# Attention and channel mix in one kernel: v products for two groups at a time, four probability buffers, one VectorE reduction per score chunk

## Chip, core and metric

The kernel runs on one core of one Trainium2 chip. The metric is the device time of one execution in microseconds, the median of several. A core has TensorE (PE, with weight loads shown apart as PEld), VectorE (DVE), ScalarE (ACT), GpSimd (POOL) and SyncE (SP, which issues every transfer here). Each engine takes its instructions in the order in which they were written and waits at semaphores.

## What is computed

Sixteen sequences of 512 tokens with 128 channels go through causal attention with 16 heads of 8 channels, a layer norm, a channel mix of the RWKV kind and a second layer norm:

```python
h = x @ W1 + b1                                   # q, k, v of 16 heads, d = 8
w = einsum('bhqd,bhkd->bhqk', q, k) / sqrt(8)
w = softmax(w * tril - (1 - tril) * 1e6)          # S = 512
x = layernorm(x + einsum('bhqk,bhkd->bhqd', w, v) @ Wp + bp)
xk = mu_k * x + (1 - mu_k) * x_prev               # xr likewise, with mu_r
out = sigmoid(xr @ W_r.T) * (relu(xk @ W_k.T) ** 2 @ W_v.T)
x = layernorm(x + out)
```

## The kernel before

**Stages and steps.** The work on one sequence passes six stages, and a step of the program works on several sequences at once, each in another stage: X (transpose x), A (q and k), S (scores with queries on the partitions, to find each row's maximum), T (the scores again with keys on the partitions, exponential, product with v), D (sums, projection, first layer norm), E (channel mix, second norm). `run_steps` runs 21 steps. A step is divided into ten groups g = 0 to 9 (two halves of five, `c` = g mod 5) and a group into four chunks i = 0 to 3. The text writes "g4" for group 4.

**A chunk.** `scores(b, par, g, i)` writes one PSUM bank of S scores (`sps`, L493, at most 512 columns in one or two matmuls, then two small mask matmuls L505 and L507) and one bank of T scores (`tps`, L473). S and T have three banks each (`BANKS = 3`). DVE reduces a bank of S to row maxima (`reduce_chunk`: L687 for chunks of one or two parts, L691 for the last group of a half). ACT turns a bank of T into probabilities (`exp_chunk_of`, L616). PE may write chunk n only once chunk n - 3 has been read. `max_unit` says which blocks an S chunk holds: a chunk with u even is one block row of 512 columns; one with u odd ("short") holds block row 2 (384 columns) and block row 0 (128 columns), which DVE reduces in two instructions.

**Masks and v.** POOL zeroes the diagonal blocks of a group's probabilities (`mask_group(b, g)`, L777, one instruction in an even c and two in the others) after the fourth exponential of the group. PE then multiplies by v (`pv(b, ..., g)`, L537, four or eight matmuls in float32, four of them side by side on strips of 32 columns), accumulating a half's five groups in the bank `ops`. `probs` has two buffers, by g mod 2. The call is at the end of each group: `pv` of group g - 1 after the chunks of group g, and `pv` of group 9 in g0 of the next step.

**The rest of the work** shares one PSUM bank, `spare`. The table `SPARE_USES[(g, place)]` sets when each use comes on PE: place 0 after chunks 0 and 1, place 1 after chunks 2 and 3. Each use waits until the one before it was read. Those that matter here:

- (0, 1) q and (1, 1) k: PE writes `spare` (L399), ACT makes the high part (L595), DVE reads `spare` once more for the rest (`qk_rest`, L715);
- (2, 0) key (L399 with `mixed`), read by ACT; (2, 1) sums1 (L440), normalised by DVE into `attn` (a reciprocal and four L725);
- (3, 0) gate (L413), read by ACT (L607); (3, 1) attnT (L443); (4, 1) value (L407); (5, 0) project; (5, 1) v;
- (6, 0) max0, (6, 1) xT, (8, 0) hT (L450), (8, 1) sums0.

**GpSimd's own order** in a step ends with: masks of g6 (L777), split of the maxima, h normalised in g7 (L804), masks of g7, the second norm's deviation, half of the result, masks of g8, the other half, `step_d` (`mix_step`, L811), masks of g9. ACT scales `step_d` twice (`scale_steps`, L633) at the end of g9, ahead of the exponentials of the next g0. In g3 POOL adds the bias to a reloaded x (`xbias`, L835), which waits for the transfer of `xres`, and stands ahead of the masks of g3.

Of the kernel before, what the change touches and what calls it, by code (L numbers as in the profile page):

```python
# [11 lines left out]
P = 128  # L12
# [10 lines left out]
QUARTET = 4  # L23
TERMS = 6 * DH
# [36 lines left out]
def bank_free(n):  # L61

    return n + 1 - BANKS

# [61 lines left out]
def diagonals(ap, u):  # L126


    if u < 2 * QUARTET:
        return ap[:, (2 if u % 2 else 3) * BLK:].rearrange("p (j w) -> p j w", w=BLK)  # L130
    return ap.rearrange("p (j w) -> p j w", w=2 * BLK)[:, :, BLK:]


def block_program(nc, x, W1, b1, Wp, bp, Wr, Wk, Wv, mu_r, mu_k, consts, half_rows, out):
    with ExitStack() as ctx:
# [96 lines left out]
        s_reduced = sem("s_reduced")  # L232
        max_high = sem("max_high")
# [139 lines left out]
        def _(pe):  # L373
# [19 lines left out]
            def rowmax_transpose(par, half):  # L393
                src = rowmax[:, par, QUARTET * half:QUARTET * half + QUARTET].rearrange("p t h a -> p (t h a)")
                return nc.tensor.transpose(spare[0:MAXIMA, 0:P], src, ident)
# [21 lines left out]
            def spare_use(b, par, g, place):  # L417
# [12 lines left out]
                elif use == "max0":  # L430
                    wait(pe, s_reduced, 4 * GROUPS * before("S", b) + 2 * GROUPS)
                    last = rowmax_transpose(1 - par, 0)
                elif use == "max1":
                    wait(pe, s_reduced, 4 * GROUPS * (before("T", b) + 1))
                    last = rowmax_transpose(par, 1)
# [85 lines left out]
            def pv(b, entries, par, g):  # L521
# [11 lines left out]
                for k in range(per_pair):  # L533
                    for t in range(QUARTET):
# [4 lines left out]
                                                probs[:, g % 2, i, off:off + w],  # L539
# [3 lines left out]
            def step(b, par):  # L543
                for g in range(GROUPS):
# [13 lines left out]
        def _(act):  # L558
# [51 lines left out]
            def exp_chunk_of(b, g, i):  # L610
                n = before("T", b)
                half, c = divmod(g, CHUNKS)
                if i == 0:
                    wait(act, pv_done, GROUPS * n + g - 1)
                wait(act, t_done, 4 * GROUPS * n + 4 * g + i + 1)
                nc.scalar.activation(probs[:, g % 2, i, :], tps[:, bank(4 * GROUPS * n + 4 * g + i), :], ACT.Exp, scale=SCALE)\  # L616
# [42 lines left out]
        def _(dve):  # L659
# [19 lines left out]
            def reduce_chunk(b, par, g, i):  # L679
# [5 lines left out]
                if u < 2 * QUARTET:  # L685
                    for t, a, off, w in max_unit(u):
                        last = nc.vector.reduce_max(rowmax[:, par, QUARTET * half + t, hh, a:a + 1],  # L687
                                                    sps[:, bank(n), off:off + w], axis=AX_X)
                else:
                    pair = QUARTET * half + max_unit(u)[0][0]  # L690
                    last = nc.vector.reduce_max(rowmax[:, par, pair:pair + 2, hh, 1],  # L691
                                                sps[:, bank(n), :].rearrange("p (j w) -> p j w", j=2), axis=AX_X)
                last.then_inc(s_reduced, 1)

# [10 lines left out]
            def spare_use(b, par, g, place):  # L705
# [11 lines left out]
                elif use in ("sums0", "sums1"):  # L717
# [43 lines left out]
        def _(pool):  # L761
# [9 lines left out]
            def mask_group(b, g):  # L771
# [3 lines left out]
                for _, _, _, off, _ in exp_chunk(g % CHUNKS, 0):  # L775
                    v = probs[:, g % 2, :, off:off + BLK]
# [128 lines left out]
```

## Time and profile before

| | |
|---|---|
| time, median of 3 | 714.41 us (711.55 to 716.44) |
| the profiled execution | 715.99 us, its span 714.3 us |
| busy in the span | PE 84%, DVE 74%, ACT 65%, POOL 61% |
| mean granted TensorE clock | 0.944 of full speed |
| 80 to 120 us and the steady steps | granted clock 1.00 |
| a steady step | 37.5 us, some of them 38 to 39 us |

The page of the profile gives sums over the whole span; the core fills up to about 120 us, has steps of equal length until about 640 us, and drains. A step is therefore read from the timeline of each engine in one stretch (394.0 to 431.5 us is used below), in which each row is one or more instructions of one kind: start, length from the first start to the last end, engine, line, what is written and read, count, and in brackets how long the engine had been idle and for whom. Records of matmuls overlap, so a PE that waits only a little shows no bracket: what tells is the distance from one row's start to the next row's.

### The profile page before, as it was taken

The page shows a single profiled execution, that of the slowest core. Times are in us where ns is not written, and L with a number is a line of the kernel's source. Part 1 is how long each engine was busy: PE and PEld are TensorE (multiplying, and loading weights), DVE is VectorE, ACT ScalarE, POOL GpSimd, SP SyncE. Part 2 cuts the span into 40 slices and gives each one's busy share as a digit, 9 for nine tenths or more (in the row PEclk, how much of TensorE's full clock was granted, in tenths as well). Part 3 has the DMA queues.
Part 4 walks back from the last instruction along what each step waited for, and adds up shares of the span by engine and source line. Part 5 has one row for each costly group of instructions (what it writes and reads, how often), then busy time and mean ns, then how long its engine had stood idle before and what let it go on. Part 6 is the DMA issues. An engine that isn't in the chain of part 4 may idle for free.

```text
span 714.3 us, 19231 instructions
## 1 busy us (share of the span) xinstructions
PE 599.9 (84%) x7405; PEld 321.4 (45%) x7405; DVE 530.4 (74%) x1388; ACT 464.6 (65%) x918; POOL 439.0 (61%) x680
## 2 busy tenths in 40 slices
PE   2359997999999999998989999899999998988623
PEld 1025453545454545454545454454545454533311
DVE  3058887889898888888898989797988888832121
ACT  1210776686878787778687777778687767676410
POOL 6110434467677676868676858576767767667653
PEclk9995899999999999999999999999999999989655
DMA  1332323132322323232323232415142332000100
GB/s 56 86 94 89 106 65 108 44 120 49 97 86 66 118 62 122 62 121 62 121 55 121 52 112 62 109 46 135 48 104 79 66 102 64 18 17 17 31 15 15
DMA packets 63615, 53.63 MB, mean 75 GB/s; under 512 B 8730, under 2 KB 59292, under 8 KB 63524
## 3 DMA queue, kind: packets, MB, share of 16 engines
q1 hardware_dynamic: 63524, 52.41, 26.2%
q8 instruction: 58, 0.95, 0.6%
q14 instruction: 33, 0.27, 0.1%
HBM read 34.82 MB, written 17.30 MB: 73 GB/s over the span
## 4 chain that ended last, share of the span: by engine, by line
PE 35%; POOL 25%; DVE 13%; ACT 11%; issue 10%; DMA 3%; SPq 2%; POOLq 0%; DVEq 0%; ACTq 0%
PE ops L537 9%; PE sps L493 7%; POOL probs L777 6%; PE spare L399 6%; ACT probs L616 5%; DVE rowmax L687 5%; POOL rstd L799 4%; POOL h L804 4%; POOL result L804 4%; PE spare L413 3%; PE spare L407 3%; PE tps L473 2%; POOL step_d L811 2%; DVE qk_rest L715 2%; DVE stats L698 2%
## 5 line engine op out<-in xcount | busy, mean ns | idle before, releaser
L616 ACT ACTIVATE probs<-tps 128x512 f32<-128x512 f32 x640 | 341.7, 598 | 125.6 <-PE tps L473 125.4
L687 DVE TENSOR_REDUCE rowmax<-sps 128x1 f32<-128x512 f32 (+2 forms) x768 | 337.7, 503 | 53.8 <-PE sps L507 52.0
L777 POOL TENSOR_SCALAR_AFFINE_SELECT probs<-probs 128x512 f32<-128x512 f32 x256 | 157.7, 633 | 157.5 <-ACT probs L616 157.0
L493 PE MATMUL sps<-kop,qop 52*128 52x384 bf16 (+3 forms) x1024 | 220.2, 310 | 34.3 <-DMA kop<-d_parts 13.8
L473 PE MATMUL tps<-qop,kop 54*128 54x128 bf16 (+3 forms) x1024 | 219.5, 304 | 12.6 <-ACT probs L616 12.6
L537 PE MATMUL ops<-probs,vop 128*32 128x384 f32 (+3 forms) x2048 | 172.7, 444 | 8.7 <-POOL probs L777 6.3
L493 PEld LDWEIGHTS sps<-kop,qop 52*128 52x128 bf16 x1024 | 71.3, 95 | 158.3 <-DVE rowmax L687 86.5
L505 PE MATMUL sps<-qmask,rows_of 64*128 64x128 bf16 (+1 forms) x640 | 134.3, 212 | 0.0
L507 PE MATMUL sps<-qmask,rows_of 64*128 64x128 bf16 (+1 forms) x640 | 131.8, 208 | 0.0
L691 DVE TENSOR_REDUCE rowmax<-sps 128x2 f32<-128x512 f32 x128 | 79.5, 684 | 13.7 <-PE sps L507 12.7
L537 PEld LDWEIGHTS ops<-probs,vop 128*32 128x32 f32 x2048 | 55.3, 110 | 73.1 <-issue 46.0
L473 PEld LDWEIGHTS tps<-qop,kop 54*128 54x128 bf16 x1024 | 69.2, 94 | 26.3 <-ACT probs L616 24.7
L507 PEld LDWEIGHTS sps<-qmask,rows_of 64*128 64x128 bf16 x640 | 62.5, 99 | 21.5 <-issue 3.4
L505 PEld LDWEIGHTS sps<-qmask,rows_of 64*128 64x128 bf16 x640 | 61.5, 97 | 16.1 <-issue 2.4
L784 POOL TENSOR_TENSOR qk_parts<-qk_rest,qk_parts 128x512 bf16<-128x512 f32 x32 | 36.8, 1152 | 35.3 <-ACT qk_parts L627 35.3
L715 DVE SCALAR_TENSOR_TENSOR qk_rest<-spare,bias,qk_parts 128x512 f32<-128x512 f32 x32 | 24.0, 751 | 29.4 <-ACT qk_parts L595 29.4
L835 POOL TENSOR_TENSOR xbias<-xres,bias 128x512 f32<-128x512 f32 x16 | 20.3, 1267 | 34.0 <-DMA xres<-L_attn_x 34.0
L817 POOL TENSOR_TENSOR mixed<-scaled,hT 128x512 f32<-128x512 f32 x32 | 40.0, 1268 | 0.8 <-ACT scaled L633 0.8
L595 ACT ACTIVATE qk_parts<-spare,bias 128x512 bf16<-128x512 f32 x32 | 21.8, 680 | 28.1 <-PE spare L399 27.5
L399 PE MATMUL spare<-xT,w1p 128*32 128x512 f32 x256 | 37.6, 662 | 2.3 <-DVE qk_rest L715 1.6
L799 POOL TENSOR_TENSOR rstd<-vareps,half_power 128x4 f32<-128x4 f32 x32 | 33.4, 1043 | 2.7
L738 DVE SCALAR_TENSOR_TENSOR gated<-gate,spare 128x512 f32<-128x512 f32 x16 | 11.0, 687 | 30.8 <-PE spare L407 30.8
(75 smaller groups left out, 650.0 us busy)
## 6 DMA issues: line engine op xcount, KB each, us to landing
d_parts<-qk_parts SPq DMA_DIRECT2D x16, 768.0 KB, 3.9
qop<-d_parts SPq DMA_DIRECT2D x192, 32.0 KB
qop<-d_parts SPq DMA_DIRECT2D x64, 96.0 KB
kop<-d_parts SPq DMA_DIRECT2D x192, 32.0 KB
kop<-d_parts SPq DMA_DIRECT2D x64, 96.0 KB
xa<-L_attn_x SPq DMA_DIRECT2D x16, 256.0 KB, 3.0
xres<-L_attn_x SPq DMA_DIRECT2D x16, 256.0 KB, 3.4
out<-result SPq DMA_DIRECT2D x16, 256.0 KB, 2.5
```

Source lines behind the costliest of these rows:

```text
L399: last = nc.tensor.matmul(spare[32 * m:32 * m + 32, :], weights[:, 32 * m:32 * m + 32], tokensT, start=True, stop=True, skip_group_check=True)
L473: last = nc.tensor.matmul(tps[:, bank(n), off:off + w], kop[r, par, pair, BLK * a:BLK * a + BLK], qop[r, par, pair, BLK * a:SEQ], start=Tr ...
L493: nc.tensor.matmul(sps[:, bank(n), off:off + w], qop[r, par, pair, BLK * a:BLK * a + BLK], kop[r, par, pair, 0:w], start=j == 0, stop=Fals ...
L505: nc.tensor.matmul(out[:, :, 0:HROWS], rows_of[r, 0, :], rhs, start=False, stop=False, skip_group_check=True)
L507: nc.tensor.matmul(out[:, :, HROWS:], rows_of[r, 1, :], rhs, start=False, stop=True, skip_group_check=True).then_inc(s_done, 1)
L537: last = nc.tensor.matmul(ops[32 * t:32 * t + 32, BLK * a:SEQ], vop[:, par, a, QUARTET * half + t, hh, :], probs[:, g % 2, i, off:off + w] ...
L616: nc.scalar.activation(probs[:, g % 2, i, :], tps[:, bank(4 * GROUPS * n + 4 * g + i), :], ACT.Exp, scale=SCALE)\
L687: last = nc.vector.reduce_max(rowmax[:, par, QUARTET * half + t, hh, a:a + 1], sps[:, bank(n), off:off + w], axis=AX_X)
L691: last = nc.vector.reduce_max(rowmax[:, par, pair:pair + 2, hh, 1], sps[:, bank(n), :].rearrange("p (j w) -> p j w", j=2), axis=AX_X)
L777: last = nc.gpsimd.affine_select(out=v, in_=v, compare_op=ALU.is_ge, fill=0.0, base=0, pattern=[[0, QUARTET], [1, BLK]], channel_multiplie ...
L799: nc.gpsimd.tensor_tensor(rstd[:, i, :], vareps[:, i, :], half_power[:], ALU.pow).then_inc(done_rstd, 1)
L804: last = nc.gpsimd.tensor_scalar(dst[:, t, :], src[:, t, :], negmean[:, i, t:t + 1], rstd[:, i, t:t + 1], ALU.add, ALU.mult)
```

## The change

1. **Product with v in pairs.** A table sets after which group which products are done: `PV_AFTER = {2: (0, 1), 4: (2, 3), 5: (4,), 7: (5, 6), 9: (7, 8)}`; that of group 9 stays in g0 of the next step. `probs` has four buffers in place of two, and the exponentials of a group wait for the product four groups back.
2. **Short S chunks** are laid out as block row 0 first, then block row 2 (384 columns), and one DVE instruction reduces the bank as four blocks of 128 columns, so that `rowmax` gets a new axis of four: blocks of a short chunk are a row's own maximum (block row 0) and three partial ones (block row 2). Once in each half, after the second chunk of its last group, a small DVE reduction over the three partial maxima of eight head rows completes them (`block2_done`), and the transposes of the maxima wait for it.
3. **attn** is made by one DVE instruction of 128x256 in place of four of 128x64.

```diff
+PBUFS = 4
+PV_AFTER = {2: (0, 1), 4: (2, 3), 5: (4,), 7: (5, 6), 9: (7, 8)}
...
-            return [(t, 2, 0, 3 * BLK), (t, 0, 3 * BLK, BLK)]
+            return [(t, 0, 0, BLK), (t, 2, BLK, 3 * BLK)]
...
-        rowmax = sb("rowmax", [P, 2, PAIRS, 2, NQBLK])
+        rowmax = sb("rowmax", [P, 2, NQBLK, PAIRS, 2, NQBLK])
...
-        probs = sb("probs", [P, 2, QUARTET, SEQ])
+        probs = sb("probs", [P, PBUFS, QUARTET, SEQ])
...
                     if g == 0 and active("D", b):
                         pv(b, before("D", b), 1 - par, GROUPS - 1)
-                    elif g > 0 and active("T", b):
-                        pv(b, before("T", b), par, g - 1)
+                    for done in PV_AFTER.get(g, ()):
+                        if active("T", b):
+                            pv(b, before("T", b), par, done)
...
                 if i == 0:
-                    wait(act, pv_done, GROUPS * n + g - 1)
+                    wait(act, pv_done, GROUPS * n + g + 1 - PBUFS)
...
-                if u < 2 * QUARTET:
-                    for t, a, off, w in max_unit(u):
-                        last = nc.vector.reduce_max(rowmax[:, par, QUARTET * half + t, hh, a:a + 1],
-                                                    sps[:, bank(n), off:off + w], axis=AX_X)
...
+                elif u % 2 == 0:
+                    last = nc.vector.reduce_max(rowmax[:, par, 0, pair, hh, 3:], sps[:, bank(n), :], axis=AX_X)
                 else:
...
+                    last = nc.vector.reduce_max(rowmax[:, par, :, pair, hh, 0],
+                                                sps[:, bank(n), :].rearrange("p (j w) -> p j w", w=BLK), axis=AX_X)
                 last.then_inc(s_reduced, 1)
+                if c == CHUNKS - 1 and i == 1:
+
+                    wait(dve, s_reduced, n - 1)
+                    of = rowmax[:, par, :, QUARTET * half:QUARTET * half + QUARTET].rearrange("p j t h a -> p a (t h) j")
+                    nc.vector.reduce_max(of[:, 2, :, 0], of[:, 0, :, 1:], axis=AX_X).then_inc(block2_done, 1)
...
-                    for t in range(TT):
-                        last = nc.vector.tensor_tensor(
-                            attn[:, t, DH * half:DH * half + DH].rearrange("q (r h) d -> q r h d", h=2),
-                            tiles[:, 0, t], inv[:, half, t].unsqueeze(3).to_broadcast([P, QUARTET, 2, DH]), ALU.mult)
-                    last.then_inc(spare_read, 1)
+                    nc.vector.tensor_tensor(
+                        attn[:, :, DH * half:DH * half + DH].rearrange("q t (r h) d -> q t r h d", h=2), tiles[:, 0],
+                        inv[:, half].unsqueeze(4).to_broadcast([P, TT, QUARTET, 2, DH]), ALU.mult).then_inc(spare_read, 1)
```

How the program reads on the engines. First TensorE, from k (`spare<-xT,w1p`, end of g1) to key (`spare<-mixed,wffT`, middle of g2), before:

```order
L399 MATMUL spare<-xT,w1p 32x512 x4
L537 MATMUL ops<-probs,vop 32x512 x4
L493 MATMUL sps<-kop,qop 128x512
L473 MATMUL tps<-qop,kop 128x512
L505 MATMUL sps<-qmask,rows_of 128x64
L507 MATMUL sps<-qmask,rows_of 128x64
L493 MATMUL sps<-kop,qop 128x512
L473 MATMUL tps<-qop,kop 128x512
L505 MATMUL sps<-qmask,rows_of 128x64
L507 MATMUL sps<-qmask,rows_of 128x64
L399 MATMUL spare<-mixed,wffT 32x512 x4
```

and now, on the same engine at the same place (line numbers are those of the changed kernel):

```order
L405 MATMUL spare<-xT,w1p 32x512 x4
L501 MATMUL sps<-kop,qop 128x512
L481 MATMUL tps<-qop,kop 128x512
L513 MATMUL sps<-qmask,rows_of 128x64
L515 MATMUL sps<-qmask,rows_of 128x64
L501 MATMUL sps<-kop,qop 128x512
L481 MATMUL tps<-qop,kop 128x512
L513 MATMUL sps<-qmask,rows_of 128x64
L515 MATMUL sps<-qmask,rows_of 128x64
L405 MATMUL spare<-mixed,wffT 32x512 x4
```

The product with v of group 0 (four matmuls) has gone from between k and key. TensorE at the end of g2, from the last short chunk to the first chunk of g3, before:

```order
L493 MATMUL sps<-kop,qop 128x384
L473 MATMUL tps<-qop,kop 128x512
L493 MATMUL sps<-kop,qop 128x128
L505 MATMUL sps<-qmask,rows_of 128x2x64
L507 MATMUL sps<-qmask,rows_of 128x2x64
L440 MATMUL spare<-cst,osum 128x128 x4
L537 MATMUL ops<-probs,vop 32x384 x4
L537 MATMUL ops<-probs,vop 32x128 x4
L493 MATMUL sps<-kop,qop 128x512
```

and now:

```order
L501 MATMUL sps<-kop,qop 128x128
L481 MATMUL tps<-qop,kop 128x512
L501 MATMUL sps<-kop,qop 128x384
L513 MATMUL sps<-qmask,rows_of 128x2x64
L515 MATMUL sps<-qmask,rows_of 128x2x64
L448 MATMUL spare<-cst,osum 128x128 x4
L545 MATMUL ops<-probs,vop 32x512 x4
L545 MATMUL ops<-probs,vop 32x384 x4
L545 MATMUL ops<-probs,vop 32x128 x4
L501 MATMUL sps<-kop,qop 128x512
```

The product of group 0 now stands here, ahead of that of group 1, and the small part of the short chunk is written first. VectorE from g6 to the end of g9 and into g0, before:

```order
L687 TENSOR_REDUCE rowmax<-sps 128x1 x16
L722 RECIPROCAL inv<-spare 128x32
L725 TENSOR_TENSOR attn<-spare,inv 128x64 x4
L691 TENSOR_REDUCE rowmax<-sps 128x2 x4
L687 TENSOR_REDUCE rowmax<-sps 128x1 x6
```

and now:

```order
L702 TENSOR_REDUCE rowmax<-sps 128x4 x2
L738 RECIPROCAL inv<-spare 128x32
L740 TENSOR_TENSOR attn<-spare,inv 128x4x64
L696 TENSOR_REDUCE rowmax<-sps 128x2 x2
L709 TENSOR_REDUCE rowmax<-rowmax 128x8
L696 TENSOR_REDUCE rowmax<-sps 128x2 x2
L699 TENSOR_REDUCE rowmax<-sps 128x1 x2
L702 TENSOR_REDUCE rowmax<-sps 128x4 x2
```

A short chunk is one reduction of 128x4 where it was two of 128x1, `attn` is one instruction, and the small reduction stands in the middle of the last group of the half.

## Rows read from the trace of the kernel before

**Rows 1.** Stretches: us, busy of PE, PEld, DVE, ACT, POOL; clock, DMA

```profile
394.01:431.48 37.47, 34.89 (x468) 19.16 (x463) 32.78 (x87) 28.78 (x58) 26.67 (x43) 1.00 0.29 85
431.48:470.28 38.80, 35.08 (x467) 19.10 (x463) 32.77 (x87) 28.78 (x58) 26.64 (x42) 1.00 0.32 88
281.17:545.42 264.25, 244.75 (x3239) 133.85 (x3235) 229.42 (x603) 201.45 (x400) 186.49 (x294) 1.00 0.32 87
```

**Rows 2.** Timeline of TensorE from k to key: start, length, what

```profile
412.12 1.06 PE L399 MATMUL spare<-xT,w1p 128*32 128x512 f32 x8
413.00 1.04 PE L537 MATMUL ops<-probs,vop 128*32 128x512 f32 x8
413.97 0.39 PE L493 MATMUL sps<-kop,qop 52*128 52x512 bf16 x1
...
414.85 1.07 PE L399 MATMUL spare<-mixed,wffT 128*32 128x512 f32 x8 [0.21 <-DVE qk_rest L715]
```

**Rows 3.** Timeline of ACT and DVE in the same stretch

```profile
413.34 0.67 ACT L595 ACTIVATE qk_parts<-spare,bias 128x512 bf16<-128x512 f32 x1
414.05 0.75 DVE L715 SCALAR_TENSOR_TENSOR qk_rest<-spare,bias,qk_parts 128x512 f32<-128x512 f32 x1 [0.50 <-ACT qk_parts L595]
```

**Rows 4.** Timeline of TensorE from attnT to the product of group 3

```profile
420.67 0.66 PE L443 MATMUL spare<-cst,attn 128*128 128x128 f32 x4
421.26 1.07 PE L537 MATMUL ops<-probs,vop 128*32 128x512 f32 x8
422.26 0.28 PE L493 MATMUL sps<-kop,qop 52*128 52x256 bf16 x1
...
424.88 1.05 PE L537 MATMUL ops<-probs,vop 128*32 128x384 f32 x16
```

**Rows 5.** Timeline of POOL, ACT and PE from g6 to the next g0

```profile
396.15 1.23 POOL L777 TENSOR_SCALAR_AFFINE_SELECT probs<-probs 128x512 f32<-128x512 f32 x2 [2.13 <-ACT probs L616]
405.17 1.03 POOL L811 TENSOR_TENSOR step_d<-hT 128x512 f32<-128x512 f32 x1
406.24 1.33 ACT L633 ACTIVATE scaled<-step_d,mus 128x512 f32<-128x512 f32 x2 [0.60 <-POOL step_d L811]
408.11 0.39 PE L473 MATMUL tps<-qop,kop 54*128 54x512 bf16 x1 [0.73 <-ACT probs L616]
```

**Rows 6.** Timeline of DVE in g6 to g8, and of PE in g9

```profile
395.91 6.74 DVE L687 TENSOR_REDUCE rowmax<-sps 128x1 f32<-128x384 f32 x16
...
404.37 0.28 PE L493 MATMUL sps<-kop,qop 52*128 52x256 bf16 x1 [0.23 <-DVE rowmax L691]
404.81 1.07 PE L537 MATMUL ops<-probs,vop 128*32 128x384 f32 x16
```

**Rows 7.** DVE's groups by shape, 281.17 to 545.42 us: busy, mean ns

```profile
L687 DVE TENSOR_REDUCE rowmax<-sps 128x1 f32<-128x512 f32 x113 | 72.5, 683 | 6.9 <-PE sps L507 6.5
L687 DVE TENSOR_REDUCE rowmax<-sps 128x1 f32<-128x384 f32 x112 | 61.2, 546 | 8.9 <-PE sps L507 8.4
L687 DVE TENSOR_REDUCE rowmax<-sps 128x1 f32<-128x128 f32 x112 | 31.3, 279 | 0.0
L725 DVE TENSOR_TENSOR attn<-spare,inv 128x64 f32<-128x64 f32 x56 | 8.6, 216 | 0.5
```

**Rows 8.** Timeline of DVE: attn, two short chunks, g4

```profile
418.11 0.61 DVE L725 TENSOR_TENSOR attn<-spare,inv 128x64 f32<-128x64 f32 x4
420.46 1.42 DVE L687 TENSOR_REDUCE rowmax<-sps 128x1 f32<-128x384 f32 x4 [0.46 <-PE sps L507]
422.80 2.48 DVE L691 TENSOR_REDUCE rowmax<-sps 128x2 f32<-128x512 f32 x4 [0.92 <-PE sps L507]
```

**Rows 9.** Waits over the span, and the timeline of one late transfer

```profile
PE ops L537 <- POOL probs L777: 6.3, 4, 3.5
...
461.14 1.29 POOL L835 TENSOR_TENSOR xbias<-xres,bias 128x512 f32<-128x512 f32 x1 [3.29 <-DMA xres<-L_attn_x]
463.65 1.07 PE L537 MATMUL ops<-probs,vop 128*32 128x384 f32 x16 [1.13 <-POOL probs L777]
```

More of the change, by code:

```diff
@@ L129, in diagonals @@
     if u < 2 * QUARTET:
-        return ap[:, (2 if u % 2 else 3) * BLK:].rearrange("p (j w) -> p j w", w=BLK)
+        blocks = ap.rearrange("p (j w) -> p j w", w=BLK)
+        return blocks[:, 0:NQBLK:3] if u % 2 else blocks[:, 3:]
     return ap.rearrange("p (j w) -> p j w", w=2 * BLK)[:, :, BLK:]
@@ L393, in rowmax_transpose @@
             def rowmax_transpose(par, half):
-                src = rowmax[:, par, QUARTET * half:QUARTET * half + QUARTET].rearrange("p t h a -> p (t h a)")
+                src = rowmax[:, par, 0, QUARTET * half:QUARTET * half + QUARTET].rearrange("p t h a -> p (t h a)")
                 return nc.tensor.transpose(spare[0:MAXIMA, 0:P], src, ident)
@@ L431, in spare_use @@
                     wait(pe, s_reduced, 4 * GROUPS * before("S", b) + 2 * GROUPS)
+                    wait(pe, block2_done, 2 * before("S", b) + 1)
                     last = rowmax_transpose(1 - par, 0)
@@ L434, in spare_use @@
                     wait(pe, s_reduced, 4 * GROUPS * (before("T", b) + 1))
+                    wait(pe, block2_done, 2 * (before("T", b) + 1))
                     last = rowmax_transpose(par, 1)
@@ L613, in exp_chunk_of @@
                 if i == 0:
-                    wait(act, pv_done, GROUPS * n + g - 1)
+                    wait(act, pv_done, GROUPS * n + g + 1 - PBUFS)
                 wait(act, t_done, 4 * GROUPS * n + 4 * g + i + 1)
-                nc.scalar.activation(probs[:, g % 2, i, :], tps[:, bank(4 * GROUPS * n + 4 * g + i), :], ACT.Exp, scale=SCALE)\
+                nc.scalar.activation(probs[:, (GROUPS * n + g) % PBUFS, i, :], tps[:, bank(4 * GROUPS * n + 4 * g + i), :], ACT.Exp, scale=SCALE)\
                     .then_inc(exp_done, 1)
@@ L684, in reduce_chunk @@
                 wait(dve, s_done, n + 1)
-                if u < 2 * QUARTET:
-                    for t, a, off, w in max_unit(u):
-                        last = nc.vector.reduce_max(rowmax[:, par, QUARTET * half + t, hh, a:a + 1],
-                                                    sps[:, bank(n), off:off + w], axis=AX_X)
-                else:
-                    pair = QUARTET * half + max_unit(u)[0][0]
-                    last = nc.vector.reduce_max(rowmax[:, par, pair:pair + 2, hh, 1],
-                                                sps[:, bank(n), :].rearrange("p (j w) -> p j w", j=2), axis=AX_X)
+                pair = QUARTET * half + max_unit(u)[0][0]
+                if u >= 2 * QUARTET:
+                    last = nc.vector.reduce_max(rowmax[:, par, 0, pair:pair + 2, hh, 1],
+                                                sps[:, bank(n), :].rearrange("p (j w) -> p j w", j=2), axis=AX_X)
+                elif u % 2 == 0:
+                    last = nc.vector.reduce_max(rowmax[:, par, 0, pair, hh, 3:], sps[:, bank(n), :], axis=AX_X)
+                else:
+                    last = nc.vector.reduce_max(rowmax[:, par, :, pair, hh, 0],
+                                                sps[:, bank(n), :].rearrange("p (j w) -> p j w", w=BLK), axis=AX_X)
                 last.then_inc(s_reduced, 1)
+                if c == CHUNKS - 1 and i == 1:
+                    wait(dve, s_reduced, n - 1)
+                    of = rowmax[:, par, :, QUARTET * half:QUARTET * half + QUARTET].rearrange("p j t h a -> p a (t h) j")
+                    nc.vector.reduce_max(of[:, 2, :, 0], of[:, 0, :, 1:], axis=AX_X).then_inc(block2_done, 1)
             def layer_norm_moments(src, i, n, ready, value, done_stats, done_moments):
```

5 lines of the change are left out of this document (3 added, 2 removed).

## Prediction

> **What bounds the kernel now.** I read the stretches first. In a steady step of 37.47 us TensorE has 34.89 us of records, VectorE 32.78, ScalarE 28.78, GpSimd 26.67, at a granted clock of 1.00, which is 2.4 GHz [rows 1]. No engine is full: VectorE has 37.47 - 32.78 = 4.7 us of idle time per step, and TensorE's figure flatters it, since its records overlap. So a sum per engine does not answer the question, and I followed one step in the timelines, asking at each place what released the instruction that everything after it stands behind. Three kinds of stretch came out.
>
> First, the chain of `spare` from k to key. PE writes k from 412.12 and is free for the next work at 413.00 [rows 2]. ACT reads it at 413.34, DVE at 414.05, done at 414.80 [rows 3]; key starts at 414.85 [rows 2]. In between PE does the product of group 0 (413.00 to 413.97) and two chunks of g2, and then still waits 0.21 us. This product lies wholly in the shadow of the chain k, ACT, DVE, key.
>
> Second, from key to the end of g5, PE's own order: sums1, the product of group 1, gate, attnT, the product of group 2 (421.26 to 422.26), g4, value, the product of group 3 at 424.88 [rows 4], project, v, the product of group 4. Here a microsecond of PE is a microsecond of the step.
>
> Third, from g6 to the next g0, GpSimd: the masks of g6 start when the exponentials of g6 are there (396.15, after 2.13 us of idleness) and GpSimd then has no gap until `step_d` ends at 405.17 + 1.03 = 406.20; ACT scales from 406.24, and only then come the exponentials of g0, so that the T matmul of its fourth chunk starts at 408.11 after 0.73 us of waiting [rows 5]. The distance 396.15 to 408.11, 11.96 us, is one chain. VectorE is nearly as tight there: 16 reductions without a gap from 395.91 for 6.74 us, and in g9 PE waits for it (404.37) before it comes to the product of group 7 [rows 6].
>
> **The change, part by part.**
>
> *Product of group 0, moved from g1 to g2.* At its old place it cost nothing. Without it PE does the two chunks of g2 about a microsecond earlier and then waits for the same `qk_rest`: key still starts at 414.85. At its new place, behind sums1, it stands in the second kind of stretch. Its price: float32 work followed by float32 work takes 412.12 to 413.00 = 0.88 us for the same number of columns, and followed by scores 413.00 to 413.97 = 0.97 or 421.26 to 422.26 = 1.00 [rows 2, 4]. In a pair the first product is of the former kind, 0.88. So **+0.88 us** per step. ACT and DVE have no work of the old shadow that could use the time: both stand in the chain.
>
> *Product of group 2, moved from g3 to g4.* g4 starts its 1.00 us earlier, value and the product of group 2 follow, and that of group 3 after 0.88 us: 0.88 - 1.00 = **-0.12 us**. Both places lie in the second stretch.
>
> *Products 5 and 7, moved from g6 to g7 and g8 to g9.* Here the third stretch decides, and PE has room: what counts is whether it comes late for GpSimd's chain. After the last chunk of a group DVE holds three banks, 3 x 0.60 = 1.8 us of work: four reductions take 2.48 us with the last one's 0.68, so they lie 0.60 apart [rows 7, 8]. A pair of products takes 0.88 + 1.00 = 1.88 us, and a chunk reaches DVE about 0.5 us after PE begins it (422.26 to 422.80 is 0.54 [rows 4, 8]). DVE idles about 0.8 us behind each pair, where a single product left it none. Walking g7 to g0 by these distances: g7 begins 1.0 us earlier and g8 0.8 us later than now, the third and fourth exponentials of g8 end about 0.1 us later, as does what GpSimd has behind the masks of g8; g9's fourth chunk starts 0.2 us later (404.6 in place of 404.37), the pair begins at 405.0 and ends at 406.9, its scores reach ACT at 407.4, and ACT is busy with `scaled` until 407.5 anyway [rows 5, 6]. The pair's second microsecond in g9 is hidden by the 0.73 us for which PE waited at 408.11 [rows 5] and by what ACT still had to do. I take **+0.1 us**; the bounds are 0 (GpSimd's chain hides all) and +1.0 (the pairs' idle times on DVE add up there, 2 x 0.8 less what DVE saves).
>
> *The short chunk's order.* Small part first puts the 384 columns behind the T matmul. Where T waits (408.11), the S part after it is 384 instead of 128 columns long: 256 columns at 2.4 GHz, **+0.1 us**. Elsewhere both row halves carry the same 512 columns.
>
> *One reduction per short chunk.* Two short chunks take 1.42 us, 0.71 with the tail; the four instructions' last is 0.28 long, so a chunk is 0.66 apart against 0.60 for one 512-column reduction [rows 7, 8]. A four-block reduction is not in the trace; the nearest is L691's two blocks, 0.60 apart like one block, and I take 0.60 (bounds 0.60 and 0.66). Sixteen short chunks a step: -0.96 us of DVE work.
>
> A page speaks against this size. The Trainium skill, "VectorE: DVE Perf Modes", section "The TRN2 errata", gives an instruction that reads PSUM a fixed 120 cycles at 0.96 GHz; by it an instruction less would be 0.125 us, the sixteen 2.0 us. The trace has 0.06 each, since an instruction starts before the one ahead has ended, and the trace decides.
>
> *attn.* Four take 0.61 us. One of 256 elements: 216 ns + 192 x (683 - 279) / 384 ns = 0.42 us [rows 7, 8]; twice, -0.38 us. *Small reduction:* 24 elements, below 0.28 us (128 elements), I take 0.17, twice, +0.34 us; its data are done two chunks earlier, so its wait costs nothing. DVE in all: -0.96 - 0.38 + 0.34 = -1.0 us of 32.8. **On the path: 0.** In the first and second stretch DVE has idle time (0.46 and 0.92 us ahead of the rows at 420.46 and 422.80 [rows 8]), in the third GpSimd's chain is as long and gets nothing. The cover is thin there, so the bound is -1.0.
>
> *Four buffers.* The exponentials' wait for the product two groups back shows nowhere; what ended ACT's idle time was T scores or, at one place, `step_d`. Worth 0. They are what lets the pairs be.
>
> *Late transfers.* The product of group 3 needs the masks of g3, which stand behind `xbias` and so behind the transfer of `xres`. Where that is late (461.14), PE waits, and the step is 38.80 us instead of 37.47; over the run 6.3 us in four places, the longest 3.5 [rows 1, 9]. SP issues the transfer at the same time as before, while PE comes to the product of group 3 later by 0.88 (product 0) and 0.88 (product 2 ahead of it), 1.76 us. That recovers 6.3 less about 1.7 of the longest, 4.6; I take **-4 us** for the run.
>
> *Sum.* +0.88 - 0.12 + 0.1 + 0.1 = 0.96 us per step in which q and k are made beside T and the channel mix's neighbours are there, 13 steps: +12.5 us. With -4 it is +8.5. The profiled execution took 715.99 us, so 724.5; it lay 1.6 us above the median of the three, so **723 us**, 1.2% slower.
>
> **The rivals.**
>
> *Faster: DVE is what paces the kernel after all.* For it: 32.78 of 37.47 us busy, no gap in g6 to g8, PE waiting for it in g9 [rows 1, 6]. Then a step loses 1.0 us of DVE work and the microsecond of product 0 lies beside it, and four pairs save 4 x 0.12 us of switching: -1.5 x 15 steps = -22, 692 us; if only the third stretch goes by DVE, half of its saving counts, about -0.5 x 14 - 4 against nothing added, 704. Against it: 4.7 us of DVE idle time per step and a GpSimd chain of 11.96 us that no part of the change shortens [rows 1, 5]. It decides if `step_d` ends with POOL having had gaps. Chance 0.20. By the page's 0.125 us per instruction the same rival would give 2.0 - 0.96 = 1.0 us more a step.
>
> *No difference: only the late transfers and a part of the microsecond.* The shadow moves: g2's chunks come earlier and the second stretch has places where PE waits a little, so that product 0 costs 0.4 rather than 0.88. (0.4 - 0.12 + 0.1) x 13 - 4 = +1, 715 us; this region, 711 to 719, gets 0.22.
>
> *Much slower: the pairs starve DVE and ACT.* If behind the pairs of g7 and g9 the idle times are not hidden (bound +1.0 above instead of +0.1): (0.96 + 0.9) x 13 - 4 = +20, 735 us. It decides if DVE's idle time behind the pair of g7 pushes sums0 later by more than GpSimd's order does. For it: the slack in my walk is only about 0.2 us. Chance 0.16.
>
> **How the numbers follow.** My forecast has 0.42, with its own range of 718 to 728. A measurement of this kernel tells about 1% from no change (the three runs span 0.7%). Over 1% faster is below 707.3: the faster rival but its edge, 0.18. Over 1% slower is above 721.6: the much slower rival and 0.32 of the forecast's 0.42, 0.48. Between: 0.34. The range for 8 in 10 leaves out the full DVE gain and the far end of starving: 704 to 733.
>
> **What the profile after would show.** Key starts as long after k as before (2.73 us), with PE idle for about a microsecond ahead of it and no product between. From key to the first chunk of g6 the step is 0.8 us longer. GpSimd still runs without a gap from the masks of g6 to `step_d`, and 12.0 to 12.2 us lie between those masks and the T matmul of g0's fourth chunk. Short chunks are reduced in 0.68 us, 0.60 apart, DVE busy near 31.8 us per step with more idle time, and PE waits for POOL ahead of a product hardly ever. A steady step is 38.4 us. I am wrong if a steady step is below 37.5 us: then a place that I took for GpSimd's or PE's was DVE's; or above 39, then the pairs starve what follows them.

## The result: 731.8 us, 2.7% slower

The changed kernel takes 731.82 us (median of four, 729.49 to 733.61), against 715.04 us for the kernel before on the same chip. The ratio is 1.0267, with a 95% interval of 1.0237 to 1.0297. The direction and the cost of moving product 0 were forecast; falls of TensorE's clock were not: +8.6 us were predicted and +16.8 came. The profiled execution took 730.78 us, its span is 728.5 us.

From the page of the changed kernel, its sums over the span:

```profile
span 728.5 us, 18909 instructions
PE 599.4 (82%) x7405; PEld 327.8 (45%) x7405; DVE 508.6 (70%) x1068; ACT 463.3 (64%) x918; POOL 439.4 (60%) x680
```

DVE has 320 instructions and 22 us of work less than before, PE the same work, and the kernel is slower. The stretches of the changed kernel from one `step_d` to the next, and a part of the second (columns as in [rows 1]):

```profile
371.71:409.97 38.26, 34.36 (x466) 19.42 (x462) 31.39 (x67) 28.71 (x58) 26.68 (x43) 1.00 0.32 85
409.97:449.87 39.90, 36.00 (x466) 19.73 (x462) 31.38 (x67) 28.71 (x58) 26.71 (x44) 0.96 0.27 83
441.20:444.70 3.50, 3.50 (x28) 1.02 (x28) 1.28 (x3) 0.57 (x1) 3.35 (x9) 0.53 0.05 9
```

There are two kinds of step. The common one takes 38.26 us; before it was 37.46 (the stretch of 37.47 in [rows 1]). The other kind takes 39.7 to 39.9 us, with the same instructions on every engine, DVE and ACT as busy as in the first kind, but the granted clock at 0.96, and at 0.53 between 441.2 and 444.7. TensorE ran there at 1.2 GHz instead of 2.4. In the kernel before, the granted clock is 1.00 from 130 to 632 us; its first fall after that (0.50 from 634 to 640 us) comes where the core already drains.

TensorE's timeline in the changed kernel, from k to the pair of g2, then the pair of g7 in either kind of step:

```profile
378.71 1.06 PE L405 MATMUL spare<-xT,w1p 128*32 128x512 f32 x8
379.71 0.39 PE L501 MATMUL sps<-kop,qop 52*128 52x512 bf16 x1
...
381.45 1.06 PE L405 MATMUL spare<-mixed,wffT 128*32 128x512 f32 x8 [1.07 <-DVE qk_rest L731]
...
383.82 1.93 PE L545 MATMUL ops<-probs,vop 128*32 128x512 f32 x24
...
397.69 0.39 PE L501 MATMUL sps<-kop,qop 52*128 52x512 bf16 x1
...
401.29 0.39 PE L501 MATMUL sps<-kop,qop 52*128 52x512 bf16 x1 [0.79 <-DVE rowmax L702]
...
402.92 1.93 PE L545 MATMUL ops<-probs,vop 128*32 128x512 f32 x24
...
441.24 3.50 PE L545 MATMUL ops<-probs,vop 128*32 128x512 f32 x24
```

Key still starts 2.74 us after k (381.45 - 378.71; 2.73 in [rows 2]), now with 1.07 us of waiting ahead of it. From key to the first chunk of g6 it is 397.69 - 381.45 = 16.24 us, against 430.37 - 414.85 = 15.52 before: +0.72. The same pair of products takes 1.93 us at 402.92 and 3.50 us at 441.24. In the profiled execution this happened five times up to 640 us, at 171.98, 441.24, 557.91, 597.43 and 635.84 us, always at the pair of g7. A sixth fall, at 654.56 us, is in the drain, at the pair of g2; every kernel here, the one before too, has falls after 626 us.

GpSimd in the changed kernel, masks of g6 and `step_d`, and DVE's two waits in that stretch:

```profile
400.93 1.23 POOL L791 TENSOR_SCALAR_AFFINE_SELECT probs<-probs 128x512 f32<-128x512 f32 x2 [2.13 <-ACT probs L625]
...
409.97 1.03 POOL L825 TENSOR_TENSOR step_d<-hT 128x512 f32<-128x512 f32 x1
```

```profile
405.26 1.29 DVE L699 TENSOR_REDUCE rowmax<-sps 128x1 f32<-128x512 f32 x2 [1.04 <-PE sps L515]
...
411.95 1.29 DVE L699 TENSOR_REDUCE rowmax<-sps 128x1 f32<-128x512 f32 x2 [0.94 <-PE sps L515]
```

GpSimd's chain is 9.04 us from masks to `step_d`, as before (9.02, [rows 5]). DVE idles a microsecond behind each of the two pairs, and these two microseconds cost nothing in this kernel. The T matmul of g0's fourth chunk starts at 412.90, 11.97 us after the masks of g6; before it was 11.96.

DVE's groups by shape in the changed kernel, 284 to 560 us:

```profile
L702 DVE TENSOR_REDUCE rowmax<-sps 128x4 f32<-128x512 f32 x116 | 74.1, 681 | 6.0 <-PE sps L515 6.0
...
L740 DVE TENSOR_TENSOR attn<-spare,inv 128x256 f32<-128x256 f32 x14 | 5.9, 425 | 0.5
...
L709 DVE TENSOR_REDUCE rowmax<-rowmax 128x8 f32<-128x24 f32 x14 | 2.7, 190 | 0.0
```

### The profile page after: what moved, and what is told of

It is laid out like the page before. It is cut to its first block, busy times and chain, and to the rows that moved or that the text cites. A ratio compares the mean times of both kernels' runs of the same rounds, so it can differ in the third digit from the quotient of the medians.

```text
span 728.5 us, 18909 instructions
## 1 busy us (share of the span) xinstructions
PE 599.4 (82%) x7405; PEld 327.8 (45%) x7405; DVE 508.6 (70%) x1068; ACT 463.3 (64%) x918; POOL 439.4 (60%) x680
## 4 chain that ended last, share of the span: by engine, by line
PE 44%; DVE 29%; ACT 9%; POOL 8%; issue 5%; DMA 3%; SPq 2%; DVEq 0%; POOLq 0%; ACTq 0%
PE ops L545 17%; DVE rowmax L699 10%; PE sps L501 8%; DVE rowmax L702 7%; PE spare L405 5%; ACT probs L625 4%; DVE stats L714 3%; PE spare L419 3%; PE spare L413 3%; PE tps L481 3%; POOL probs L791 2%; DVE rowmax L696 2%; DVE qk_rest L731 2%; ACT qk_parts L604 2%; DVE moments L718 1%
## 5 line engine op out<-in xcount | busy, mean ns | idle before, releaser
L501 PE MATMUL sps<-kop,qop 52*128 52x128 bf16 (+3 forms) x1024 | 222.2, 311 | 50.0 <-DVE rowmax L702 12.7
L699 DVE TENSOR_REDUCE rowmax<-sps 128x1 f32<-128x512 f32 x256 | 164.5, 684 | 91.7 <-PE sps L515 91.7
L702 DVE TENSOR_REDUCE rowmax<-sps 128x4 f32<-128x512 f32 x256 | 163.7, 682 | 11.7 <-PE sps L515 11.6
L545 PE MATMUL ops<-probs,vop 128*32 128x384 f32 (+3 forms) x2048 | 165.0, 452 | 3.7 <-POOL probs L791 3.7
L501 PEld LDWEIGHTS sps<-kop,qop 52*128 52x128 bf16 x1024 | 71.5, 95 | 144.0 <-DVE rowmax L702 43.5
L545 PEld LDWEIGHTS ops<-probs,vop 128*32 128x32 f32 x2048 | 61.7, 113 | 94.4 <-issue 76.0
L696 DVE TENSOR_REDUCE rowmax<-sps 128x2 f32<-128x512 f32 x128 | 82.1, 684 | 0.7
L515 PEld LDWEIGHTS sps<-qmask,rows_of 64*128 64x128 bf16 x640 | 62.8, 99 | 37.7 <-issue 6.1
L405 PE MATMUL spare<-xT,w1p 128*32 128x512 f32 x256 | 38.4, 676 | 2.4 <-DVE qk_rest L731 1.6
L405 PE MATMUL spare<-mixed,wffT 128*32 128x512 f32 x128 | 18.8, 661 | 21.1 <-DVE qk_rest L731 12.8
```

Source lines behind the costliest of these rows:

```text
L405: last = nc.tensor.matmul(spare[32 * m:32 * m + 32, :], weights[:, 32 * m:32 * m + 32], tokensT, start=True, stop=True, skip_group_check=True)
L501: nc.tensor.matmul(sps[:, bank(n), off:off + w], qop[r, par, pair, BLK * a:BLK * a + BLK], kop[r, par, pair, 0:w], start=j == 0, stop=Fals ...
L515: nc.tensor.matmul(out[:, :, HROWS:], rows_of[r, 1, :], rhs, start=False, stop=True, skip_group_check=True).then_inc(s_done, 1)
L545: last = nc.tensor.matmul(ops[32 * t:32 * t + 32, BLK * a:SEQ], vop[:, par, a, QUARTET * half + t, hh, :], probs[:, (GROUPS * entries + g) ...
L696: last = nc.vector.reduce_max(rowmax[:, par, 0, pair:pair + 2, hh, 1], sps[:, bank(n), :].rearrange("p (j w) -> p j w", j=2), axis=AX_X)
L699: last = nc.vector.reduce_max(rowmax[:, par, 0, pair, hh, 3:], sps[:, bank(n), :], axis=AX_X)
```

## The experiments

Every kernel ran beside the kernel before. The length of a step is the distance between two starts of `step_d` in a profiled execution. Beside the changed kernel the kernel before took 715.04 us, beside experiments 1 to 4 712.23, beside 5 to 8 713.95, beside 9 and 10 713.24; so across these groups the ratios compare better than the times.

**1. Products alone again, all else kept.**

```diff
-PV_AFTER = {2: (0, 1), 4: (2, 3), 5: (4,), 7: (5, 6), 9: (7, 8)}
+PV_AFTER = {1: (0,), 2: (1,), 3: (2,), 4: (3,), 5: (4,), 6: (5,), 7: (6,), 8: (7,), 9: (8,)}
```

> The changed kernel with its table set back to one product per group, at the ends of g1 to g9 as before; the DVE changes, the short chunks' order and the four buffers stay. My theory (product 0 out of the shadow of k and key, plus TensorE's clock at 1.2 GHz in five places at the paired products of g7; DVE's saving hidden): a steady step of 37.5 us, no fall of the clock in the steady steps, 714 us (712 to 717). Rival, DVE paces the kernel: 1.0 us less a step, 700 us. Rival, the new order of the short chunk or the small reduction costs: over 720 us.

Measured: 718.58 us, ratio to before 1.0086 (1.0044 to 1.0127). The step is 37.52 us:

```profile
370.00 1.03 POOL L825 TENSOR_TENSOR step_d<-hT 128x512 f32<-128x512 f32 x1
407.53 1.03 POOL L825 TENSOR_TENSOR step_d<-hT 128x512 f32<-128x512 f32 x1
```

Without the pairs 1.8 of the 2.7% are gone (13 us of 17 by the medians), and in the steady steps the clock does not fall. DVE's microsecond per step is worth nothing at this placement: 37.52 is no less than 37.46. The time is 4.6 us above what I expected. The kernel is still 0.9% (6 us) slower than the one before, although the steps account for 0.06 us each; experiments 7 and 10 come back to it.

**2. Pairs alone, on the kernel before.** `PV_AFTER` and the four buffers put into the kernel before; DVE as before.

```diff
-probs = sb("probs", [P, 2, QUARTET, SEQ])
+probs = sb("probs", [P, PBUFS, QUARTET, SEQ])
...
-                    elif g > 0 and active("T", b):
-                        pv(b, before("T", b), par, g - 1)
+                    for done in PV_AFTER.get(g, ()):
+                        if active("T", b):
+                            pv(b, before("T", b), par, done)
```

> The kernel before with nothing but the pairs and the four probability buffers. My theory: all of the loss comes with the pairs, so a steady step of 38.2 us, falls of the clock at the pair of g7, and 731 us (727 to 735) or a few us more, since DVE is 1.0 us slower per step. Rival, the loss is the DVE part's: 715 us. Rival, DVE's saving is worth something once PE feeds it in bursts: 740 us or more.

Measured: 744.56 us, ratio 1.0465 (1.0406 to 1.0525), the third reading. A step without a fall of the clock is 38.7 us against 38.26 with the new DVE part, and there were seven falls between 200 and 640 us instead of four. DVE's timeline in this kernel, its waits behind the pair of g4 and behind the pair of g7 in a step with a fall:

```profile
403.95 1.29 DVE L692 TENSOR_REDUCE rowmax<-sps 128x1 f32<-128x512 f32 x2 [1.30 <-PE sps L511]
...
417.48 2.66 DVE L692 TENSOR_REDUCE rowmax<-sps 128x1 f32<-128x512 f32 x6 [2.59 <-PE sps L511]
```

DVE idles 1.30 us behind the pair of g4 (1.21 in the changed kernel, at 393.66), and 2.59 us behind that of g7, since the pair itself runs at half the clock. The value of DVE's saving depends on where TensorE's bursts are: nothing with single products, 0.44 us per step and three falls of the clock with pairs. My expectation (731, or a few more) missed this.

**3. Product 0 back between k and key, pairs at g4, g7, g9.**

```diff
-PV_AFTER = {2: (0, 1), 4: (2, 3), 5: (4,), 7: (5, 6), 9: (7, 8)}
+PV_AFTER = {1: (0,), 2: (1,), 4: (2, 3), 5: (4,), 7: (5, 6), 9: (7, 8)}
```

> The changed kernel with product 0 alone put back to the end of g1, where it stands between k and key; pairs at g4, g7, g9 stay. My theory: 0.7 us per step come back, the step is 37.5 us, the clock still falls at g7 in some steps at 1.6 us each: 719 us (715 to 723). Rival, pairs as such starve DVE and ACT: the step stays at 38.0 or more, 726 us or more.

Measured: 719.18 us, ratio 1.0101 (1.0049 to 1.0153); steps of 37.40 to 37.6 us, and two falls of the clock before 640 us, both after 580 us. The pairs of g4, g7 and g9 do not lengthen a step. The expectation held, 719 us and 37.5 us a step.

**4. The pair of g7 apart.** Product 5 at the end of g6, product 6 at g7; product 0 stays moved.

```diff
-PV_AFTER = {2: (0, 1), 4: (2, 3), 5: (4,), 7: (5, 6), 9: (7, 8)}
+PV_AFTER = {2: (0, 1), 4: (2, 3), 5: (4,), 6: (5,), 7: (6,), 9: (7, 8)}
```

> The changed kernel with the pair of g7 taken apart alone: product 5 back at the end of g6, product 6 at the end of g7. My theory: the step stays 38.2 us, since product 0 is still out of the shadow, but TensorE works through g6 and g7 as before and its clock stays at 2.4 GHz in the steady steps: 723 us (720 to 726), five falls at 1.6 us gained. Rival, the falls come from the kernel's slower pace as a whole: they stay, 731 us.

Measured: 722.52 us, ratio 1.0157 (1.0112 to 1.0202). The steps are 38.24 us, all of them, and the clock is whole from 120 to 640 us:

```profile
120.00:640.00 520.00, 465.29 (x6258) 260.26 (x6258) 426.97 (x896) 387.04 (x770) 357.74 (x567) 1.00 0.31 82
```

That is 9.3 us less than the changed kernel by the medians, and 1.1% (7.9 us) by the ratios, with the same regular step; five falls at 39.90 - 38.26 = 1.64 us would be 8.2.

**5. Only product 0 moved.**

```diff
-PV_AFTER = {1: (0,), 2: (1,), 3: (2,), 4: (3,), 5: (4,), 6: (5,), 7: (6,), 8: (7,), 9: (8,)}
+PV_AFTER = {2: (0, 1), 3: (2,), 4: (3,), 5: (4,), 6: (5,), 7: (6,), 8: (7,), 9: (8,)}
```

> The changed kernel with only product 0 out of place: pair of products 0 and 1 at the end of g2, every other product alone at the end of the group behind it. It differs from the run with all products alone in this one move. My theory: the step is longer by 0.85 us (0.88 for the product less the switching saved at the pair, which has no place here), 38.3 us, no fall of the clock, and one late transfer in the fill less: 723 us against 718.6 with all alone. Rival, the move costs nothing by itself and the loss needs the pairs of g4, g7 and g9: 718 us, a step of 37.5.

Measured: 726.20 us, ratio 1.0168 (1.0121 to 1.0215). The step is 38.43 us:

```profile
373.41 1.03 POOL L825 TENSOR_TENSOR step_d<-hT 128x512 f32<-128x512 f32 x1
411.84 1.03 POOL L825 TENSOR_TENSOR step_d<-hT 128x512 f32<-128x512 f32 x1
```

38.43 - 37.52 = 0.91 us for one product moved by one group, 0.88 by the prediction. With the pairs of g4 and g9 in place as well the step is 38.24 (experiment 4), 0.19 less; 0.12 was predicted for the pair of g4. The whole is 7.6 us slower than experiment 1, where 723 us was expected: 12 steps of 0.91 are 10.9, and the fill is 1.9 us shorter (the first `step_d` at 142.06 instead of 144.00).

**6. More work for TensorE.** The changed kernel with the transposes of xT, which stand ahead of g7, done twice.

```diff
-                    for t in range(TT):
+                    for t in 2 * list(range(TT)):
                         last = nc.tensor.transpose(spare[:, P * t:P * t + P], xa[:, t, :], ident)
```

> The changed kernel with the four transposes of xT at the end of g6 done twice (0.6 us more of TensorE work in each step, ahead of g7, where TensorE waits for VectorE; nothing else is changed). If the falls of the clock at the pair of g7 come from how little TensorE does in g6 and g7, they go away in the steady steps and the kernel is faster with more work: step 38.3 us throughout, 725 us (722 to 728). If they have nothing to do with it, the time is 731.8 us or up to 0.6 us a step more, 740.

Measured: 726.93 us, ratio 1.0203 (1.0160 to 1.0246), 4.9 us faster than the changed kernel by the medians and 0.6% (4.6 us) by the ratios, with 0.43 us more of TensorE work in each step that has the transposes. They take 1.09 us instead of 0.66, TensorE's wait behind them shrinks from 0.79 to 0.35 us, steps are 38.29 us (one of 38.8), and from 120 us on the clock does not fall before 632 us:

```profile
401.35 1.09 PE L431 MATMUL spare<-cst,xa 128*128 128x128 f32 x8
...
403.17 0.39 PE L501 MATMUL sps<-kop,qop 52*128 52x512 bf16 x1 [0.35 <-DVE rowmax L702]
...
120.00:640.00 520.00, 471.16 (x6307) 268.22 (x6299) 424.03 (x893) 385.77 (x768) 355.70 (x563) 1.00 0.31 82
```

So the pair of g7 alone does not bring the falls: it is still there. What goes with them is how long TensorE waits for DVE ahead of it. From about 560 us on no sequence is left to transpose, and the wait is 1.32 us, in this kernel too; the changed kernel's row:

```profile
595.81 0.39 PE L501 MATMUL sps<-kop,qop 52*128 52x512 bf16 x1 [1.32 <-DVE rowmax L702]
```

The kernels with a pair in g7 and no product at the end of g6 (the changed one and experiments 2, 3 and 6) can be counted together, 13 steps of each from the first `step_d` on:

| wait ahead of the pair of g7 | kernels | steps | falls |
|---|---|---|---|
| 0.35 us | 6 | 11 | 0 |
| 0.79 us | changed, 3 | 22 | 3, all in the changed kernel |
| 0.96 us | 2 | 11 | 6 |
| 1.32 to 1.39 us | all four | 8 | 6 |

One fall of this kernel is left, at 633.28 us, in a step without transposes. The counts come from one profiled execution of each kernel.

**7. Big part of the short chunk first**, on experiment 1.

```diff
-            return [(t, 0, 0, BLK), (t, 2, BLK, 3 * BLK)]
+            return [(t, 2, BLK, 3 * BLK), (t, 0, 0, BLK)]
```

> All products alone as in the first experiment, and the short chunk's 384 columns issued ahead of its 128 as before the change, with the layout and the single reduction kept. My theory: the small part first costs up to 0.1 us per step at the T matmul that waits in g0: step 37.46 instead of 37.52, 717.5 us against 718.6. Rival, the order is what makes the DVE part slower than before by 0.9%: 712 us.

Measured: 715.89 us over ten runs, ratio 1.0028 (1.0008 to 1.0048); step 37.50 instead of 37.52. The difference to experiment 1, 2.7 us by the medians and 0.6% (4 us) by the ratios, is larger than 12 steps of 0.02 us explain. The intervals of the two ratios overlap (1.0044 to 1.0048), so a part or all of it may be scatter; what the order is worth is not settled.

**8. Product 4 one group later, a pair at g7.** On experiment 1 (the copy of the first half's sums goes to g7 with it).

```diff
+PV_AFTER = {1: (0,), 2: (1,), 3: (2,), 4: (3,), 6: (4,), 7: (5, 6), 8: (7,), 9: (8,)}
...
-                    if g == CHUNKS + 1 and active("T", b):
+                    if g == CHUNKS + 2 and active("T", b):
                         copy_o(before("T", b), 0, last_use(b, "sums0"))
```

> A use of the four buffers by my theory of the path: products 0 to 3 alone at the ends of g1 to g4, product 4 moved from the end of g5 to the end of g6, where GpSimd's chain is what all wait for, products 5 and 6 at the end of g7, 7 and 8 alone; the copy of the first half's sums (ScalarE) moves from g6 to g7. Theory: 0.98 us of TensorE work leave the path ahead of g6, and the exponentials of g6 end up to 0.5 us earlier without the copy ahead of them; VectorE's work in g6 to g9 becomes the bound for a part of it. Step 36.3 us (36.0 to 36.8), 702 us (698 to 708). Rival, the kernel is paced elsewhere: 37.5 and 718, or with the clock falling at the pair of g7, 722.

Measured: 716.79 us, ratio 1.0027 (0.9999 to 1.0056), steps of 37.68. 702 us was expected. Where the step is bound shows in DVE's rows: from y in g5 on DVE has no gap up to the pair of g7, and in the kernel before none from y (390.29) into g9. DVE's timeline in experiment 8:

```profile
350.55 0.69 DVE L747 TENSOR_TENSOR y<-spare,xbias 128x512 f32<-128x512 f32 x1
...
358.41 1.28 DVE L702 TENSOR_REDUCE rowmax<-sps 128x4 f32<-128x512 f32 x2
360.87 1.29 DVE L699 TENSOR_REDUCE rowmax<-sps 128x1 f32<-128x512 f32 x2 [1.18 <-PE sps L515]
```

Here DVE waits 1.18 us behind the pair of g7. That this wait lengthens the step, because the path now goes by DVE as well as by GpSimd, is my reading; experiment 9, which has no pair there but moves other products too, has a step 0.71 us shorter.

**9. Every product of the second half of the step one group later, none in pairs** (called f5 below). Experiment 7 with the table below, product 8 in the middle of the next g0, where PE waits for ACT, and the copy of the first half's sums at g7 as in experiment 8.

```diff
+PV_AFTER = {1: (0,), 2: (1,), 3: (2,), 4: (3,), 6: (4,), 7: (5,), 8: (6,), 9: (7,)}
...
+                        if g == 0 and i == 1 and active("D", b):
+                            pv(b, before("D", b), 1 - par, GROUPS - 2)
```

> Products 0 to 3 alone at g1 to g4; 4, 5, 6, 7 alone at the ends of g6, g7, g8, g9 (one group later than before); product 8 in the middle of g0 of the next step, where TensorE waits for ScalarE; 9 at the end of g0; the copy of the first half's sums at g7; DVE as in the changed kernel, big part of the short chunk first. In the run before this one DVE had no gap from y in g5 (350.55) until the pair of g7, GpSimd's chain began 0.9 us earlier after y, and the pair of g7 then cost 1.2 us. Theory: from y on the path goes by DVE and GpSimd together; without a pair both chains are shorter by 0.65 us (DVE) and 0.9 us (GpSimd), a step of 36.8 us (36.5 to 37.1), 707 us. Rival, DVE's saving never reaches the end: 37.5 us, 715.

Measured: 706.08 us, ratio to before 0.9887 (0.9838 to 0.9935), steps of 36.97 us.

> The same places of the products as in f5_one_group_later on the kernel before, DVE's instructions as before. If the path from y on goes by DVE, this kernel has 0.6 us more of it per step than f5: step 37.4 us, 714 us, and the DVE part of the change is worth 7 us here, where it was worth nothing with the products of before. Rival: GpSimd's chain alone decides, and both are at 36.6 us, 704.

The same places with DVE's instructions of before: 706.34 us, ratio 0.9899 (0.9842 to 0.9956), step 37.10 us. The prediction for this kernel failed (714): DVE's saving is worth 0.13 us per step here, not 0.6. What brought the gain are four buffers used to move products off the path (and the copy that moved with them), not the reductions.

**10. The transfer of xres at the start of a step**, on experiment 9 (f5) and on experiment 7 (e7).

```diff
                 other = 1 - par
+                if active("D", b):
+                    wait(sp, xbias_done, before("D", b))
+                    sp.dma_start(xres[:], x[b + OFFSET["D"]].rearrange("(t p) e -> p t e", p=P)).then_inc(xres_in, 16)
                 if active("S", b):
...
-                if active("D", b):
-                    wait(sp, xbias_done, before("D", b))
-                    sp.dma_start(xres[:], x[b + OFFSET["D"]].rearrange("(t p) e -> p t e", p=P)).then_inc(xres_in, 16)
```

> f5_one_group_later with the transfer of xres issued at the start of each step instead of behind the loads of the maxima. GpSimd's xbias no longer waits 2 us for it. Theory: the masks of g3 come earlier and the late steps (0.5 to 1.3 us each) and the wait of 3.5 us in the fill go: 3 to 5 us less than f5, 703 us. Rival: the transfer collides with the loads of operands that now run beside it, no gain.

> e7_big_part_first with the transfer of xres issued at the start of each step. This measures the term of late transfers by itself: 4 us less than 715.9, 712 us, no step longer than 37.6 and the first full step 1.0 us shorter. Rival: in most executions no transfer is late, the term is below 1 us, and the profiled execution of before was an unlucky one.

Measured: on experiment 9, 700.47 us, ratio 0.9808 (0.9754 to 0.9862), the fastest kernel here; on experiment 7, 709.22 us, ratio 0.9938 (0.9907 to 0.9970), 6.7 us less than experiment 7. Its steady step is 37.49 (37.50 in experiment 7), and no step from the second on is late any more, where experiment 7 had two of 37.7. Most of the gain lies in the fill, 6.3 us. The first full step was expected 1.0 us shorter and is not: 38.26 against 38.28. The first `xbias` of experiment 7, and then of the same kernel with the early transfer:

```profile
122.33 1.26 POOL L849 TENSOR_TENSOR xbias<-xres,bias 128x512 f32<-128x512 f32 x1 [5.56 <-DMA xres<-L_attn_x]
```

```profile
115.98 1.27 POOL L849 TENSOR_TENSOR xbias<-xres,bias 128x512 f32<-128x512 f32 x1
```

The first `step_d` comes at 144.0 us in experiment 1, at 139.6 in the changed kernel and at 136.3 with the early transfer. The kernel before had it at 141.5, so that 2.5 us of the difference between experiment 1 and before are in a fill whose scatter I cannot separate from an effect of the DVE part.

## Why the prediction was wrong

**Right: the product out of the shadow.** Predicted +0.88 - 0.12 up to g6, measured +0.72 in the changed kernel. Alone it is 0.91 (experiment 5), and putting it back takes 0.7 to 0.9 off (experiment 3, 37.4 to 37.6 us). The whole step was predicted at 38.4 us and is 38.26.

**Right: the third stretch.** GpSimd's chain hides the pairs of g7 and g9. For them and for the short chunk's order +0.1 us each was predicted, 12.0 to 12.2 us from the masks of g6 to g0's fourth T matmul; it is 11.97 after 11.96, so neither shows there. DVE's idle times behind the pairs, 0.8 predicted, are 1.04 and 0.94.

**Right for this placement: DVE's saving is worth 0.** No step became shorter by it: 37.52 us in experiment 1, 37.50 in 7, 37.46 before. The reductions take 681 ns, attn 425 ns, the small one 190 ns, against 0.68, 0.42 and 0.17. The sum on DVE, 32.78 to 31.39, is -1.39 us with -1.0 predicted. A part of the difference, 2 x 0.07 us, is the small reduction: its 190 ns overlap its neighbours, so that it takes 0.10 us of DVE's time (409.73 - 409.63) where I had 0.17, as DVE's timeline of the changed kernel shows:

```profile
409.63 0.19 DVE L709 TENSOR_REDUCE rowmax<-rowmax 128x8 f32<-128x24 f32 x1
409.73 1.28 DVE L696 TENSOR_REDUCE rowmax<-sps 128x2 f32<-128x512 f32 x2
```

**Right in sign, too large: late transfers.** Predicted -4, from 6.3 us that PE waited for the masks. The same row of the waits in the changed kernel:

```profile
PE ops L545 <- POOL probs L791: 3.7, 4, 1.8
```

By this measure 2.6 us are recovered: the wait of 3.54 us in the fill is 1.27, the two in the steady steps (0.27 and 1.13) are gone, and those in the drain are longer. By lengths, the kernel before has 3.0 us beyond 37.46 in the twelve steps from the first `step_d` on, but 1.0 of that is in its first step, which is long in every kernel, with the early transfer too (38.26 against 37.49 us). Its fill is 1.9 us longer than that of the changed kernel; that can't be put down to the transfer alone, since its clock is at 0.50 from about 54 to 77 us and again about 127, and in the changed kernel only from about 66 to 75.

**Wrong: the clock.** The sum priced everything at the granted clock of 1.00, since no steady step of before had another. The step that failed is the one on products 5 and 7, "PE has room: what counts is whether it comes late for GpSimd's chain". I counted the room as harmless. Without product 5 at the end of g6, TensorE has only 0.66 us of transposes and four chunks ahead of the pair, with a wait for DVE of 0.79 us among them (401.29), and in some steps the clock is then at 1.2 GHz for the pair: 3.50 us instead of 1.93. The three falls in steady steps cost 1.64, 1.58 and 1.43 us; against the steps of experiment 4, which has none, the first of the five cost 1.6 and the last 1.4. That is +7.6 us that the sum does not have. Both ways to give TensorE work there take falls away: experiment 4 all five (1.1%), experiment 6 the three in steps with transposes, and one of the two behind them, where its edit changes nothing (0.6% in all); and the counts under experiment 6 show more falls the longer the wait.

The two profiled spans differ by 14.2 us, and their steps say where: 12 steps x 0.80 = +9.6, four falls and a long first step +7.2, what the kernel before has beyond 37.46 per step -3.0, fill -1.9, what follows the twelfth step +2.3 (it holds the fifth fall). This is an account of two executions, read from the same rows, and not a test. The medians differ by 16.8.

**The rivals.** "Faster" fell with experiment 1. "The pairs starve DVE" had the place right and the price for this kernel wrong, but experiment 2 shows a case in which a part of it holds: with DVE's instructions of before the step is 38.7 us, 0.44 longer, where the rival added 0.9. "No difference" had product 0 cost 0.4 us; it costs 0.91.

**What stays open.** The wait makes the falls likelier, but does not decide which step has one: TensorE's rows ahead of the pair at 441.24 lie 38.26 us behind those ahead of 402.92, the same waits of 0.79 us among them, and only one of the two pairs fell. What the DVE part, the short chunk's order and the buffers cost by themselves is not settled either: 0.9% in experiment 1 (1.0044 to 1.0127), 0.3% with the old order in experiment 7 (1.0008 to 1.0048), where their steps are longer than before by only 0.06 and 0.04 us. The sum had 1.3 us for the order and nothing for the rest.

## What to carry to other kernels

Before work is moved for the sake of fewer switches, look at what it covered: a product that stood between the links of a chain through three engines cost nothing there and 0.9 us behind them (experiments 1 and 5). A burst of TensorE work needs work ahead of it as well: where the move leaves TensorE waiting, look at the granted clock of each step rather than at its mean, because under a fall the matmuls take about twice as long (3.50 us for 1.93 here). And deeper buffers pay when they let work move into a stretch that another engine decides, one group later and not in pairs.

## What the runs showed of the hardware

I had not expected that a TensorE with 34 us of records in a step of 38 would ever be given half its clock, nor that 0.43 us of redundant transposes per step could make the kernel 0.6% faster. The Trainium skill, "TensorE: Matmul & The Clock Gate", section "What's actually happening", says that the gate has two states and none between; the trace agrees: the granted clock reads 0.50 from 441.4 to 444.0 us and 1.00 from 444.5 on, and the 0.53 of the stretch shown above is a mean over both.

The reduction of 512 columns takes the same time with one, two and four outputs per partition (684, 684 and 681 ns in the changed kernel). The product of 256 elements from PSUM took 425 ns; the same skill, "VectorE: DVE Perf Modes", section "The TRN2 errata", gives (N + 151) / 0.96 ns for a float32 `tensor_tensor` add, checked there at 512 and 2048 elements. For 256 that is 424 ns, an estimate: this product with one input in PSUM agrees.
